# Second cross-attention: which engine rounds the scaled values, and which copies a third turned tile

## The reference

```python
def _L1_xattn_ref(x, cond, Wq, bq, Wkv, bkv, Wp, bp):
    H, hd = 16, 16
    q = (x @ Wq + bq).reshape(1, B * N, H, hd)
    kv = (cond @ Wkv + bkv).reshape(1, -1, 2, H, hd)
    k, v = kv[:, :, 0], kv[:, :, 1]
    ...
    q = _fq_sym(q, axis=-1)          # round(x / s) * s, s = max|x| / 127
    k = _fq_sym(k, axis=-1)
    v = _fq_sym(v, axis=2)           # one scale per channel, over all 4096 rows
    attn = softmax(q @ k^T)          # 16 heads of 256 x 4096
    attn = _fq_unsigned(attn, axis=-1)   # round to 0..255 of the row's maximum
    out = attn @ v
    return out.reshape(B, N, C) @ Wp + bp
```

## Time and profile before

| | us |
|---|---|
| median of 3 runs | 698.17 |
| lowest and highest of them | 696.98, 699.37 |
| the profiled execution, its own time | 695.71 |
| its span in the trace | 693.6 |
| the fourteen heads 1 to 14 of the stage | 164.01 |

### The profile page before, as it was taken

How to read it: one execution, slowest core, us unless ns; L and a number is a source line. 1 busy time by engine, 2 the same in 40 slices (tenths; PEclk the granted TensorE clock), 3 DMA queues, 4 the chain that set the end, 5 groups by cost and what they waited for, 6 DMA issues and landing times. The chain is left out here.

```text
span 693.6 us, 12664 instructions
## 1 busy us (share of the span) xinstructions
PE 600.2 (87%) x4667; PEld 400.9 (58%) x4667; DVE 480.4 (69%) x776; ACT 388.7 (56%) x746; POOL 329.3 (47%) x263
## 2 busy tenths in 40 slices
PE   4976899997899999888964898888878878989996
PEld 3532445444777777666740565656555655757774
DVE  4257999995766654566776999999999945342221
ACT  4227975552432221356874999999999934032221
POOL 1019999994223330033605888998999810000000
PEclk9998999999999999999975887887898879999999
DMA  8526500001846663034465789887889629600000
GB/s 336 244 73 260 228 0 1 0 1 50 297 137 199 187 176 124 16 114 145 143 167 145 161 138 165 153 164 159 150 170 173 101 56 423 291 1 1 0 0 16
DMA packets 97664, 93.07 MB, mean 134 GB/s; under 512 B 70659, under 2 KB 88387, under 8 KB 93702
## 3 DMA queue, kind: packets, MB, share of 16 engines
q1 hardware_dynamic: 84928, 85.93, 45.7%
q10 hardware_dynamic: 12678, 6.36, 3.2%
HBM read 68.78 MB, written 6.62 MB: 109 GB/s over the span
## 5 line engine op out<-in xcount | busy, mean ns | idle before, releaser
L2095 DVE TENSOR_REDUCE d_nmax<-d_psum 128x1 f32<-128x1024 f32 x128 | 152.2, 1214 | 5.6 <-PE d_psum L2251 5.5
L2251 PE MATMUL d_psum<-kst,qT 96*128 96x512 bf16 x256 | 95.4, 472 | 33.4 <-ACT d_e L2192 12.7
L529 POOL TENSOR_TENSOR b_h<-b_h,b_cb 128x1024 f32<-128x1024 f32 x32 | 88.0, 2749 | 6.5 <-DVE b_h L579 6.1
L2075 POOL TENSOR_SCALAR d_rounded<-d_e,d_lift 128x1024 f16<-128x1024 f32 x64 | 72.4, 1131 | 13.4 <-issue 7.4
L2192 ACT ACTIVATE d_e<-d_psum,d_nmax 128x1024 f32<-128x1024 f32 x64 | 71.3, 1118 | 13.2 <-DVE d_nmax L2095 12.2
L2075 POOL TENSOR_SCALAR d_rounded<-spare,d_lift 128x1024 f16<-128x1024 f32 x62 | 70.1, 1131 | 15.0 <-ACT d_lift L2196 10.7
L579 DVE TENSOR_TENSOR_SCAN b_h<-b_dA,b_psum 128x1024 f32<-128x1024 f32 x32 | 73.2, 2286 | 2.5 <-ACT b_dA L634 2.0
L2192 ACT ACTIVATE spare<-d_psum,d_nmax 128x1024 f32<-128x1024 f32 x64 | 71.4, 1120 | 1.9 <-DVE d_nmax L2095 1.9
L634 ACT ACTIVATE b_dA<-b_dtT,b_A 128x248 f32<-128x248 f32 x128 | 53.7, 490 | 33.1 <-DVE b_h L579 28.1
L2278 PEld LDWEIGHTS d_psum<-d_ident_f,d_rounded 128*128 128x128 f16 x512 | 45.1, 122 | 32.0 <-issue 20.0
L690 PE MATMUL b_psum<-b_bdiag,b_dtx 128*128 128x512 f32 x128 | 60.2, 594 | 0.8 <-DVE b_h L579 0.8
(11 more groups left out here) (428 smaller groups left out, 1188.7 us busy)
## 6 DMA issues: line engine op xcount, KB each, us to landing
c_w<-in_w0gu SPq DMA_DIRECT2D x16, 768.0 KB, 5.0
kst<-kT_scratch SPq DMA_DIRECT2D x84, 128.0 KB, 2.8
w<-in_w SPq DMA_DIRECT2D x8, 1088.0 KB, 21.0
b_cb<-c_scratch SPq DMA_DIRECT2D x4, 2048.0 KB, 7.1
c_w<-in_w0dn SPq DMA_DIRECT2D x16, 384.0 KB, 5.8
kT_scratch<-k_kT ACTq DMA_DIRECT2D x15, 384.0 KB, 2.8
a_ctx<-in_ctx SPq DMA_DIRECT2D x2, 2048.0 KB, 19.7
k_ctxT<-in_ctxT SPq DMA_DIRECT2D x12, 256.0 KB, 3.1
```

The source lines that it names most:

```text
L529: nc.gpsimd.tensor_tensor(hv, hv, cv, ALU.mult).then_inc(hc_ready, 1)
L2075: nc.gpsimd.tensor_scalar(tile_of(r, j), e[j], lift[t][:, f:f + 1], HALF_ULP_ONE, ALU.mult, ALU.add).then_inc(r_ready, 1)
L2095: nc.vector.tensor_reduce(nm[:, t, m:m + 1, f:f + 1], quarter(m, j).unsqueeze(1), AX.X, ALU.max, negate=True).then_inc(nm_ready, 1)
L2251: last = nc.tensor.matmul(quarter(m, j)[:, b * 512:(b + 1) * 512], qT[0:QROWS, m:m + 1, t * P:(t + 1) * P], kst[m % 2][0:QROWS, at:at + 51 ...
```

## The change

GpSimd rounds the scaled values of head m, between its quarters 5 and 6 of that head, with the constant in a tile of one column (`d_rounder`) that it sets at the start of the stage. VectorE no longer rounds them. The tiles that TensorE turned are split anew: VectorE copies 4 and 6 of the even heads and 4, 6 and 7 of the odd heads, ScalarE 5 and 7 of the even heads and 5 of the odd heads. Both engines' copies count in one semaphore each, and TensorE waits by a count over heads of unequal length.

```diff
-    EVEN = tuple(j for j in BY_PE if j % 2 == 0)
-    ODD = tuple(j for j in BY_PE if j % 2 == 1)
+    BY_VECTOR = ((4, 6), (4, 6, 7))
+    BY_SCALAR = tuple(tuple(j for j in BY_PE if j not in own) for own in BY_VECTOR)
...
+        rounder = sb("d_rounder", [P, 1])
...
+                nc.gpsimd.memset(rounder[:, :], ROUND).then_inc(rounder_ready, 1)
...
+                def round_values(m, s):
+                    if m == 0:
+                        pool.wait_ge(rounder_ready, 1)
+                    if m >= 2:
+                        pool.wait_ge(av_done, m + 1)
+                    pool.wait_ge(vhf_ready, m + 1)
+                    nc.gpsimd.tensor_scalar(vh[s][:, :, :], vhf[s][:, :, :], rounder[:, 0:1], -ROUND, ALU.add, ALU.add)\
+                      .then_inc(vh_ready, 1)
+
                 def round_head(m, s):
...
                         t, f = j // QT, j % QT
+                        if j == APH - 2:
+                            round_values(m, s)
...
-                def round_values(m):
-                    s = m % 2
-                    dve.wait_ge(vhf_ready, m + 1)
-                    if 2 <= m < H:
-                        dve.wait_ge(av_done, m + 1)
-                    nc.vector.tensor_scalar(vh[s][:, :, :], vhf[s][:, :, :], ROUND, ROUND, ALU.add, ALU.subtract)\
-                      .then_inc(vh_ready, 1)
...
-                        if j in EVEN and 1 <= m < H + 1:
-                            copy_even(m, j)
+                        if 1 <= m < H + 1 and j in BY_VECTOR[(m - 1) % 2]:
+                            copy_turned(m, j)
                         if j == 2 and 2 <= m < H + 2:
                             finish(m)
-                        if j == APH - 1 and m < H:
-                            round_values(m)
...
-                        if j in ODD and 1 <= m < H + 1:
-                            copy_odd(m, j)
+                        if 1 <= m < H + 1 and j in BY_SCALAR[(m - 1) % 2]:
+                            copy_turned(m, j)
```

More of the change, by code:

```diff
@@ L1967, in xattn1_stage @@
         turned_in = [sem(f"d_turned_in{u}") for u in range(2)]
-        even_copied = sem("d_even_copied")
-        odd_copied = sem("d_odd_copied")
+        vector_copied = sem("d_vector_copied")
+        scalar_copied = sem("d_scalar_copied")
+        rounder_ready = sem("d_rounder_ready")
         av_done = sem("d_av_done")
@@ L2007, in head_cols, with count, wait_copied @@
             return slice(h * HD, (h + 1) * HD)
+        def count(copies, heads):
+            return sum(len(copies[h % 2]) for h in range(heads))
+        def wait_copied(eng, h, j):
+            for copied, copies in ((vector_copied, BY_VECTOR), (scalar_copied, BY_SCALAR)):
+                if j in copies[h % 2]:
+                    eng.wait_ge(copied, count(copies, h) + copies[h % 2].index(j) + 1)
         def tile_of(a, j):
@@ L2100, in search, with copy_turned @@
                                                 accum_out=mb[:, t, m, QT - 1:QT]).then_inc(mb_ready, 1)
-                def copy_even(m, j):
+                def copy_turned(m, j):
                     t, f = j // QT, j % QT
@@ L2107, in copy_even @@
                     nc.vector.tensor_scalar(pT[1 - m % 2][:, t, f * CPQ:(f + 1) * CPQ, :].rearrange("p c q -> p (c q)"),
-                                            turn_tile(m, j), -HALF_ULP_ONE, None, ALU.add).then_inc(even_copied, 1)
+                                            turn_tile(m, j), -HALF_ULP_ONE, None, ALU.add).then_inc(vector_copied, 1)
                 def finish(m):
@@ L2197, in exps, with copy_turned @@
                                              bias=mb[:, t, m:m + 1, QT - 1]).then_inc(lift_ready, 1)
-                def copy_odd(m, j):
+                def copy_turned(m, j):
                     t, f = j // QT, j % QT
@@ L2204, in copy_odd @@
                     nc.scalar.activation(pT[1 - m % 2][:, t, f * CPQ:(f + 1) * CPQ, :].rearrange("p c q -> p (c q)"),
-                                         turn_tile(m, j), ACT.Copy, bias=-HALF_ULP_ONE).then_inc(odd_copied, 1)
+                                         turn_tile(m, j), ACT.Copy, bias=-HALF_ULP_ONE).then_inc(scalar_copied, 1)
                 def round_last():
@@ L2263, in bank_free @@
                         if before != "values" and 1 <= back <= H:
-                            copied, some = ((even_copied, EVEN), (odd_copied, ODD))[before % 2]
-                            pe.wait_ge(copied, (back - 1) * len(some) + some.index(before) + 1)
+                            wait_copied(pe, back - 1, before)
                             return
@@ L2290, in values @@
                     else:
-                        pe.wait_ge(even_copied, m * len(EVEN) - len(EVEN))
-                        pe.wait_ge(odd_copied, m * len(ODD) - len(ODD))
+                        pe.wait_ge(vector_copied, count(BY_VECTOR, m - 1))
+                        pe.wait_ge(scalar_copied, count(BY_SCALAR, m - 1))
                     for b in range(NKC):
```

## The result

The changed kernel takes 716.65 us (four runs, 715.64 to 720.73) against 698.77 us for the kernel before on the same chip: a ratio of 1.0258, 95% interval 1.0234 to 1.0282, some 18 us slower. The forecast was 697.8 us, with a range up to 702.0. The measured time lies 14.6 us above the end of that range.

The account below looks back on a forecast made before the run. VectorE was taken to bound the kernel, with the bound moving to GpSimd. Terms -11.1 (waits) - 0.75 (collisions) + 10.5 (new roundings) + 0.5 (remaining waits) + 0.5 (tail) = -0.35 us, giving 697.8 us; range 694.3 to 702.0.

Parts of the forecast that it names:

- GpSimd becomes the bound at its own work plus the slot: Heads of the second cross-attention: GpSimd's 10.98 us plus 0.70 for the new rounding gives 11.68 us per head, above VectorE's 11.05.
- Step (c): GpSimd's new rounding: a slot of 0.70 us, bounds 0.60 to 1.36, fifteen of them adding 10.5 us.
- Rival 2: GpSimd's new rounding costs like a two-input instruction, 1.36 us: +9.9 us, 707.7 us; chance 0.05.
- The rest of the sum: GpSimd's queue: lift waits go, -11.1 us; groups stretched by VectorE's rounding go back, -0.75; remaining waits and tail, +0.5 each.
- Step (e): GpSimd's waits: chains through keys and through turns have slack of 2.4 and 3 us; 0.5 us allowed for remaining waits.
- the chain through the keys: From GpSimd's roundings over SP's key loads and scores to lift: 16.1 us against 18.6 until needed, slack 2.4 us.
- What makes it wait is VectorE: Kernel before, heads: GpSimd's waits for lift, 11.1 us in sum, come from VectorE, whose queue has no room left.
- Rival 4: VectorE remains the bound and its relief shows in full over 14 heads: -5.2 us, 693.0 us; chance 0.05.
- Step (f): Start of the stage: VectorE's wait of 5.79 us goes, but only gives it a lead, not a gain of 5.8 us.
- Step (g): Tail, head 15: VectorE's sums stand behind its copy of tile 7, delaying the copy of outputs by 0.5 us.

Follow-up runs that it names:

- e2: Changed kernel with GpSimd's new instruction as mult and add instead of add and add, so no rounding to whole numbers; 701.34 us, ratio 1.0030.
- e14: Changed kernel with GpSimd rounding by two converting copies, f32 to int16 to f16; 707.68 us, ratio 1.0137.
- e3: Changed kernel with GpSimd rounding by two instructions of mult and add; 714.42 us, ratio 1.0224.
- e4: Changed kernel without the new instruction: GpSimd's scaling writes f16 directly, values not rounded to whole numbers; 698.0 us, ratio 0.9976.
- e13: e4 with SP issuing the keys of head m+2 ahead of the transposes of head m; 690.49 us, ratio 0.9877.
- e6: Changed kernel's new split of copies alone, with VectorE still rounding the values and GpSimd not; 703.07 us, ratio 1.0070.
- e8: e4 without TensorE's 32 correction products per head; 692.69 us, ratio 0.9918.
- e12: Kernel before, with VectorE's rounding of a head's values moved behind quarter 2 of the next head; 699.79 us, ratio 1.0022.
- e15: Kernel before with both edits, keys first (e10) and VectorE's rounding behind quarter 2 of the next head (e12); 697.25 us, ratio 0.9970.
- e10: Kernel before, with SP issuing the keys of head m+2 ahead of the transposes of head m; 697.69 us, ratio 0.9995.
- e1: Kernel before, unchanged, with eighteen instruction forms timed on GpSimd behind its end; at 128x512 add+add took 2.00 us, mult+add 0.69.
- e9: Kernel before, with twelve more instruction forms timed on GpSimd behind its end; mult+add pairs 0.69 us, other pairs 1.9 to 2.0.

## Why the prediction was wrong, point by point

**GpSimd becomes the bound at its own work plus the slot: right.** The head is 11.02 us plus the slot at four prices (e2, e14, e3, the changed kernel), and GpSimd's waits for lift vanish at the three higher ones.

**Step (c), the price: wrong, and this is the miss.** The term 15 x 0.70 = 10.5 us is 15 x 2.09 = 31.4 us. Both ends of the bound were drawn from neighbours that share the shape: the upper one, a two-input instruction, 1.36 us, was taken as safe. What should have been noticed is that no row of the trace before has GpSimd with a pair of adds; line 2075 was called the "same operation", when only the instruction's name and operands were the same. Even for mult+add the slot was low, 0.79 and not 0.70: the fixed part, 94 ns from memsets, is 0.69 - 0.43 = 0.26 us. Rival 2 had the right mechanism, a dear insert, at 0.05 and at half of its size.

**The rest of the sum: about right.** Along GpSimd's queue, from its first rounding to quarter 4 of head 15, the time went from 182.1 us to 574.74 - 371.75 = 203.0 us, +20.9. The sum with the measured slot is -11.1 - 0.75 + 31.4 = +19.5; where the other 1.4 us come from isn't shown.

**Step (e), slack and waits.** With the slot at 0.79 (e2), 2.5 us of waits remain where 0.5 were allowed. The slack of 2.4 us in the chain through the keys was worked out rightly as far as GpSimd's pace stays over 11.7 us. Its meaning was missed. The chain spans two heads, so 2.4 us are 1.2 us per head: by this estimate it closes at about 10.5 us in the mean, and it needs little on top to reach 11.7. What comes on top, late loads or the lower clock of TensorE, is argued and not shown. Shown is that without VectorE's rounding the head is 11.75 us (e4), and 11.24 us once the keys go first (e13). The chain was as near to the bound as VectorE.

**"What makes it wait is VectorE": half right.** e6 shows that VectorE's queue is a bound: 4.2 us added to it cost 3.4 to 6.4 us. But e4 takes 0.5 us per head off it and gains nothing in the heads. Rival 4, VectorE's relief in full at 693 us, is wrong even for a free insert. The kernel before is held by two limits at nearly the same 11.7 us, VectorE's queue and the keys behind the transposes, with TensorE's work beside the latter (e8).

**Step (f)**, no gain from the wait at the start of the stage: right for the kernel before (e12). With the keys first the lead seems to pay: heads 1 and 2 take 22.27 us in e15 and 24.32 in e10, in one profile of each.

**Step (g), the tail: wrong.** From GpSimd's quarter 4 of head 15 to the last copy of outputs it is 563.63 - 554.85 = 8.78 us before and 582.94 - 574.74 = 8.20 us after: 0.6 us less, not 0.5 more. From there to the addition of the result it is 4.60 us before and 5.25 us after, at a granted clock of 0.55 and 0.50, and no term held that clock. Together 13.38 and 13.45 us: that nothing was lost is two differences that cancel. VectorE's timeline at the end of the changed kernel, which answers to the earlier trace rows:

```profile
580.01 0.69 DVE L2131 TENSOR_SCALAR d_probsT<-d_psum 128x1024 f16<-128x1024 f16 x1 [0.27 <-PE d_psum L2291]
580.62 0.28 DVE L2156 TENSOR_TENSOR d_zpart<-d_zpart,d_dm 128x128 f32<-128x128 f32 x1
...
588.19 0.69 DVE L2185 TENSOR_TENSOR x_residual<-x_residual,d_psum 128x512 f32<-128x512 f32 x1 [4.24 <-PE d_psum L2340]
```

The sums do run behind the copy as foretold, and the copy of outputs right behind them. But the copy of tile 7 itself comes earlier, 5.27 us behind GpSimd's quarter 4 in place of 6.23, and the collision with GpSimd's last roundings is gone (2.33 us, not 2.89).

**What stays open.** Why add and add is slow on GpSimd isn't shown, only that it is so for the pair and for each element. How much of e4's remaining 11.7 us per head is TensorE's lower clock and how much its work wasn't separated: e8 takes work away, not clock. And e3's median lies 5 us above what its heads, against those of the changed kernel, would give. In the two profiles that difference lies outside the stage, 2.0 us ahead of GpSimd's first rounding and 2.4 us behind the addition of the result, in code that both share; why isn't known.

## What to carry to other kernels

Before work is moved to another engine, look for a row of that engine with the same pair of operations, not only with the same instruction and shape; where there is none, the cost has no upper bound from the trace, and the instruction alone, behind an unchanged kernel, settles it. When an engine is full, a second limit can lie right behind it: ask of each chain what its pace would be if the full engine were free, before counting a relief as a gain. An issue that waits behind another in one DMA queue inherits the waits of that other; putting the one that can go first in front cost nothing here (e10) and became worth something once the first limit fell (e13).

## What the runs showed of the hardware that was not expected

- On GpSimd a one-input instruction of 128x512 f32 takes 0.62 us (mult+add, two immediates), 0.69 us (mult+add, add+mult, mult+mult with a pointer), 0.61 us (converting copy), 1.49 to 1.57 us (one operation alone) and 1.92 to 2.02 us (add+add, add+subtract, mult+subtract, subtract+mult, max+min) (e1, e9). One operation costs over twice what the right two cost.
- Rounding f32 to whole numbers in f16 costs GpSimd 2.09 us of its queue by add and add, 1.58 by two passes of mult and add (e3) and 1.36 by two conversions over int16 (e14).
- The first rounding of GpSimd in the stage starts between 371.35 us (e14) and 376.42 us (e9), in profiled executions whose code up to there is the same but for one small memset. That is as much as many of the effects above, and the reason to read heads rather than totals.
- The last products of the stage follow the granted clock: from the last copy of outputs to the addition of the result it is 2.82 us at a granted 1.00 (e10), 4.60 us at 0.55 (before) and 5.25 us at 0.50 (the changed kernel).
